# Attention in an eight-stage kernel: one output product for two heads, with row sums spread by TensorE

## The reference

```python
kv = _rmsnorm(k_pass_lat, kv_a_ln_w) @ kv_b_proj_w.T          # latent: 64 wide
scores = jnp.einsum('bhqd,bhkd->bhqk', q, k) * scaling
scores = jnp.where(causal[None, None], scores, NEG)
probs = jax.nn.softmax(scores.astype(jnp.float32), axis=-1).astype(q.dtype)
out = jnp.einsum('bhqk,bhkd->bhqd', probs, v)
out = out.transpose(0, 2, 1, 3).reshape(b, s, H * V_DIM)
return out @ o_proj_w.T
...
x = _layernorm(x + _L0_attn_ref(x, ...), axis=-1)
```

## Time and profile before

| | |
|---|---|
| Median of 3 runs | 815.58 us (813.26 to 816.98) |
| Span of the profiled execution, first to last instruction | 851.6 us |
| Mean granted TensorE clock | 0.982 |
| TensorE, VectorE, ScalarE, GpSimd busy | 92%, 65%, 46%, 32% |
| Attention loop in the profiled execution | about 72 to 413 us |

### The profile page before, as it was taken

The page is one execution under the profiler, slowest core; times in us unless marked ns, Lnnn a source line. Parts: engine busy times, 40 slices in busy tenths (PEclk is TensorE's granted clock), DMA queues, the critical chain, the costliest instruction groups (busy, mean ns, idle before and its releaser), DMA issues.

```text
span 851.6 us, 16159 instructions
## 1 busy us (share of the span) xinstructions
PE 786.6 (92%) x4635; PEld 660.7 (78%) x4635; DVE 556.9 (65%) x1423; ACT 394.8 (46%) x898; POOL 271.2 (32%) x357
## 2 busy tenths in 40 slices
PE   8998999999899999999879998899999799999957
PEld 7887877778787887777677877788897688888746
DVE  4324778877778787777345555468856387778536
ACT  1334656656565666655123343323333266666411
POOL 2004445534333232222345545524415100000241
PEclk9999999999999999999889999999999999999979
DMA  7449950000000000073176999687621335555321
GB/s 212 102 107 384 406 198 34 34 27 27 21 27 28 20 21 14 27 240 135 51 230 184 323 319 296 213 288 257 246 99 69 106 112 150 149 149 153 95 69 49
DMA packets 62881, 120.74 MB, mean 142 GB/s; under 512 B 18272, under 2 KB 32864, under 8 KB 62688
## 3 DMA queue, kind: packets, MB, share of 16 engines
q1 hardware_dynamic: 51824, 95.41, 35.2%
q0 software_dynamic: 7680, 21.51, 7.0%
q10 hardware_dynamic: 3312, 3.02, 1.0%
HBM read 76.13 MB, written 43.78 MB: 141 GB/s over the span
## 4 chain that ended last, share of the span: by engine, by line
PE 65%; DVE 11%; issue 11%; ACT 4%; POOL 3%; another core or an unknown queue 3%; DMA 2%; DVEq 0%; SPq 0%; ACTq 0%; POOLq 0%
PE scores L1627 9%; PE scores L1625 8%; PE scores L1626 8%; PE scores L1849 5%; PE acc_ps L2035 4%; PE misc_ps L1755 3%; PE probsT_ps L1762 3%; PE probsT_ps L1740 3%; PE misc_ps L1753 3%; DVE xT_lo L1096 3%; PE scores L1859 3%; PE acc_ps L1740 2%; PE probsT_ps L1979 2%; DVE neg_max L1090 2%
## 5 line engine op out<-in xcount | busy, mean ns | idle before, releaser
L826 ACT ACTIVATE area<-scores,neg_max 128x128 f32<-128x128 f32 (+7 forms) x128 | 94.9, 742 | 87.7 <-DVE neg_max L1090 85.5
L1090 DVE TENSOR_REDUCE neg_max<-scores 128x1 f32<-128x128 f32 (+7 forms) x128 | 95.8, 750 | 22.1 <-PE scores L1712 20.8
L708 POOL DMA_INDIRECT xe_d<-x_rows,send_i x64 | 64.1, 1001 | 55.5 <-ACT x_rows L850 38.5
L738 POOL DMA_INDIRECT ye_d<-area,home_i x64 | 61.4, 959 | 58.7 <-issue 28.6
L1849 PE MATMUL scores<-area 128*96 128x128 f32 x512 | 69.1, 279 | 2.1 <-issue 1.3
L1625 PE MATMUL scores<-kT_hi,weff_hi 128*128 128x512 f32 (+3 forms) x172 | 66.8, 388 | 0.9 <-ACT area L803 0.4
L1849 PEld LDWEIGHTS scores<-area 128*96 128x96 f32 x512 | 60.5, 166 | 5.2 <-issue 2.7
L1627 PE MATMUL scores<-kT_hi,weff_lo 128*128 128x512 f32 (+3 forms) x172 | 61.7, 359 | 0.0
L1626 PE MATMUL scores<-kT_lo,weff_hi 128*128 128x512 f32 (+3 forms) x172 | 61.5, 358 | 0.0
L696 POOL CAST weff_hi<-area 128x256 fp32r<-128x256 f32 x42 | 17.0, 406 | 136.5 <-PE scores L1712 88.8
L1755 PE MATMUL misc_ps<-xT_lo,xT_hi 128*128 128x512 f32 x144 | 58.4, 406 | 2.2 <-DVE xT_lo L1096 2.1
(11 more groups left out here) (290 smaller groups left out, 2081.4 us busy)
## 6 DMA issues: line engine op xcount, KB each, us to landing
area<-w SPq DMA_DIRECT2D x23, 512.0 KB, 4.0
area<-gate_up SPq DMA_DIRECT2D x24, 384.0 KB
xe_d<-area SPq DMA_DIRECT2D x8, 1088.0 KB, 11.3
ye_d<-area SPq DMA_DIRECT2D x8, 1024.0 KB, 16.7
area<-w SPq DMA_DIRECT2D x8, 1024.0 KB, 7.2
area<-ye_d SPq DMA_DIRECT2D x15, 512.0 KB, 5.2
area<-xe_d SPq DMA_DIRECT2D x28, 272.0 KB
area<-down SPq DMA_DIRECT2D x24, 192.0 KB
```

Source lines behind the costliest of these rows:

```text
L826: act.activation(row_of(n)[:, 0:L], score_bank(n)[:, 0:L], ACT.Exp, bias=neg_max[:, n % 4:n % 4 + 1], accum_out=rsum[:, s, k:k + 1]).then_ ...
L1090: dve.tensor_reduce(neg_max[:, n % 4:n % 4 + 1], score_bank(n)[:, 0:(n // HEADS + 1) * P], AX.X, ALU.max, negate=True).then_inc(max_ready, 1)
```

## The change

- `wvo` holds each head once: two neighbouring heads lie one above the other in its 128 rows (8 x 256 columns in place of 16 x 256).
- Once ScalarE has copied the context, VectorE adds the halves (`sum_context`): for heads 0 and 2 of a group into rows 0 to 63 of `ctxS`, for heads 1 and 3 into rows 64 to 127. Each of the two instructions has 64 partitions and 256 columns, one operand in PSUM and one in SBUF. This stands first in slot 0 two groups later.
- The division by the row sum moves ahead of the output product. `invert` writes each inverse in 64 copies (128 x 4 x 64), last in slot 3 of the group's own slots. TensorE transposes these copies (two transposes of 128x128, `spread_shares`, a new tenant of the PSUM seats) in slot 1 of the next group, ScalarE copies the result to SBUF (`copy_shares`, slot 2), and GpSimd multiplies `ctxS` by it (`share`, slot 1 of the group after).
- One output for a group: two products of 128 rows and 256 columns into one bank, in slot 2 two groups later. VectorE adds it to the residual with one plain addition in slot 3 (`add_out`).
- The copied context has one buffer in place of two; the context bank is free for the next group when the halves are added. Some semaphores are merged to make room for new ones.

The core of the diff:

```diff
-        wvo = cutA3(HEADS * HID)
+        wvo = cutA3(PAIRS * HID)
+        ctxS, shares = cutA3(3, HID), cutA3(3, HID)
+        rinv = cutA3(2, QUAD, RANK)
...
-                if spot % 2 and 0 <= G - 2:
-                    tenants.append(("out", QUAD * (G - 2) + spot // 2))
-        tenants += [("out", QUAD * (GROUPS - 1) + i) for i in range(QUAD)]
+                if spot == 3 and 0 <= G - 1 < GROUPS:
+                    tenants.append(("shares", G - 1))
+                if spot == 5:
+                    tenants += [("out", g) for g in outs_at(G)]
+        tenants += [("out", g) for g in outs_at(GROUPS + 1)]
...
+            def share(g):
+                pool.wait_ge(ctx_summed, 2 * g + 2)
+                pool.wait_ge(shares_done, g + 1)
+                pool.tensor_tensor(ctxS[:, g % 3, :], ctxS[:, g % 3, :], shares[:, g % 3, :], ALU.mult).then_inc(ctx_shared, 1)
...
             def copy_ctx(G):
                 act.wait_ge(ctx_step, blocks_to(G + 1))
-                if G >= 2:
-                    act.wait_ge(out_ready, QUAD * (G - 1))
-                act.copy(ctxT[:, G % 2, :], ctx_ps[:]).then_inc(ctx_copied, 1)
+                act.copy(ctxT, ctx_ps[:]).then_inc(ctx_copied, 1)
+
+            def copy_shares(g):
+                act.wait_ge(shares_ps, g + 1)
+                if g >= 3:
+                    act.wait_ge(ctx_shared, g - 2)
+                act.copy(shares[:, g % 3, :], seat_of("shares", g)[:, 0:HID]).then_inc(shares_done, 1)
...
-                dve.tensor_copy(wvo[:, bass.ds(2 * m * HID, 2 * HID)], misc[:]).then_inc(wvo_done, 1)
+                for b in range(2):
+                    ins = dve.tensor_copy(wvo[b * RANK:(b + 1) * RANK, bass.ds(m * HID, HID)],
+                                          misc[b * RANK:(b + 1) * RANK, b * HID:(b + 1) * HID])
+                ins.then_inc(wvo_done, 1)
...
-                dve.reciprocal(rinv[:, G % 3, :], rsum[:, G % 3, :]).then_inc(rinv_done, 1)
+                if G >= 2:
+                    dve.wait_ge(shares_ps, G - 1)
+                dve.reciprocal(rinv[:, G % 2], rsum[:, G % 3, :].unsqueeze(2).broadcast_to([P, QUAD, RANK])).then_inc(rinv_done, 1)
+
+            def sum_context(g):
+                dve.wait_ge(ctx_copied, g + 1)
+                if g >= 3:
+                    dve.wait_ge(out_ready, g - 2)
+                for b, other in ((0, 1), (1, 0)):
+                    mine_, its = (slice(k * RANK, (k + 1) * RANK) for k in (b, other))
+                    dve.tensor_tensor(ctxS[mine_, g % 3, :].rearrange("p (a n) -> p a n", a=2),
+                                      ctx_ps[mine_, :].rearrange("p (a b n) -> p a b n", a=2, b=2)[:, :, b, :],
+                                      ctxT[its, :].rearrange("p (a b n) -> p a b n", a=2, b=2)[:, :, b, :],
+                                      ALU.add).then_inc(ctx_summed, 1)
...
-                dve.scalar_tensor_tensor(x1[:, t, :], out_of(n), rinv[:, s, k:k + 1], x1[:, t, :] if h else x_in[:, t, :],
-                                         ALU.mult, ALU.add).then_inc(out_read, 1)
+                dve.tensor_tensor(x1[:, t, :], out_of(g), x_in[:, t, :] if first else x1[:, t, :],
+                                  ALU.add).then_inc(out_read, 1)
...
-                behind = n - 1 - 2 * QUAD
-                if 0 <= behind < TILES * HEADS:
-                    add_head(behind)
+                if i == 0 and 0 <= G - 2 < GROUPS:
+                    sum_context(G - 2)
+                if i == QUAD - 1:
+                    for g in outs_at(G):
+                        add_out(g)
...
-                if i == 1 and 0 <= G - 1 < GROUPS:
-                    invert(G - 1)
+                if i == QUAD - 1 and G < GROUPS:
+                    invert(G)
...
                     if G:
-                        pe.wait_ge(ctx_copied, G)
+                        pe.wait_ge(ctx_summed, 2 * G)
...
+            def spread_shares(g):
+                pe.wait_ge(rinv_done, g + 1)
+                take_seat("shares", g)
+                for a in range(2):
+                    last = pe.transpose(seat_of("shares", g)[:, a * P:(a + 1) * P],
+                                        rinv[:, g % 2, 2 * a:2 * a + 2].rearrange("p b r -> p (b r)"), ident[:])
+                last.then_inc(shares_ps, 1)
+
+            def output(g):
+                pe.wait_ge(ctx_shared, g + 1)
+                take_seat("out", g)
+                m = g % SETS * 2
+                for a in range(2):
+                    last = pe.matmul(out_of(g), ctxS[:, g % 3, a * P:(a + 1) * P], wvo[:, (m + a) * HID:(m + a + 1) * HID],
+                                     start=a == 0, stop=a == 1)
+                last.then_inc(out_ready, 1)
```

More of the change, by code:

```diff
@@ L109, in build @@
         rsum = sb("rsum", [P, 3, QUAD])
-        rinv = sb("rinv", [P, 3, QUAD])
         y = sb("y", [P, HID])
         sgd = sb("sgd", [P, 2, BANK])
-        ctxT = sgd
+        ctxT = sgd[:, 0, :]
         stats = sb("stats", [P, 6])
@@ L235, in build @@
         ld_head = [sem(f"ld_head{u}") for u in range(2)]
-        consts, made = sem("consts"), sem("made")
-        x_split, kv_ready, sq_done, keys_done, kT_ps, k_split, lat_split = (
-            sem(n) for n in ("x_split", "kv_ready", "sq_done", "keys_done", "kT_ps", "k_split", "lat_split"))
+        made = sem("made")
+        x_split, kv_ready, keys_done, kT_ps, k_split, ctx_summed, ctx_shared = (
+            sem(n) for n in ("x_split", "kv_ready", "keys_done", "kT_ps", "k_split", "ctx_summed", "ctx_shared"))
+        shares_ps, shares_done = sem("shares_ps"), sem("shares_done")
         weff_ps, weff_f32, weff_split, wvo_ps, wvo_done, qT_ps, qT_done = (
@@ L250, in build @@
         block = ctx.enter_context(nc.Block())
-        rows_zeroed, homes_made, home_step, home_done = (
-            sem(n) for n in ("rows_zeroed", "homes_made", "home_step", "home_done"))
+        rows_zeroed, home_step, home_done = (sem(n) for n in ("rows_zeroed", "home_step", "home_done"))
         zeroed, x1T_psd, x1T_done, logits_done, logits_read, chosen_done, place_done, place_read, send_done = (
@@ L401, in route_at, with out_slot, outs_at @@
             return route_places.get((G % SETS, place)) if SETS + 2 <= G < GROUPS else None
+        def out_slot(g):
+            return g + 2
+        def outs_at(G):
+            return [g for g in range(GROUPS) if out_slot(g) == G]
         tenants = []
@@ L418, in build @@
         LENT = pT + [acc, half[3]] + half[0:3]
-        long_rows = seat("out", TWO_OUTS)
+        long_rows = seat("block", blocks_to(SHORT // QUAD - 2))
         tail = seat("block", blocks_to(GROUPS - 1))
@@ L719, in pool_slot @@
                     split_q(n // 2 + 3)
+                if i == 1:
+                    for g in outs_at(G):
+                        share(g)
                 t, at = divmod(n - 2 * HEADS, HEADS)
                 if t == 0 and at == 0:
-                    pool.wait_ge(homes_made, 2)
+                    pool.wait_ge(consts1, 6)
                     pool.wait_ge(rows_zeroed, 16 * ROWS_ZEROED)
@@ L819, in exp_probs @@
                 if n == 4:
-                    act.wait_ge(lat_split, 2)
+                    act.wait_ge(keys_done, TILES + 3)
                 if row_before(n) >= 0:
@@ L855, in act_slot @@
             def act_slot(G, i, n):
+                if i == 2 and 0 <= G - 1 < GROUPS:
+                    copy_shares(G - 1)
                 for place in (2 * i, 2 * i + 1):
@@ L1027, in _ @@
             shared_act(1)
-            act.wait_ge(consts1, 6)
+            act.wait_ge(consts1, 8)
             for t in range(TILES // 2, TILES):
@@ L1100, in invert, with add_out @@
                 dve.wait_ge(probs_ready, QUAD * (G + 1))
-                dve.reciprocal(rinv[:, G % 3, :], rsum[:, G % 3, :]).then_inc(rinv_done, 1)
[L1103 to L1108, removed]
+                if G >= 2:
[11 more added lines that the diff above has]
+                                      ALU.add).then_inc(ctx_summed, 1)
+            def add_out(g):
+                t, first = g // SETS, g % SETS == 0
+                dve.wait_ge(out_ready, g + 1)
+                if first:
                     dve.wait_ge(ld_x, 32)
-                    dve.wait_ge(rinv_done, n // QUAD + 1)
                 else:
-                    dve.wait_ge(out_read, n)
-                dve.scalar_tensor_tensor(x1[:, t, :], out_of(n), rinv[:, s, k:k + 1], x1[:, t, :] if h else x_in[:, t, :],
-                                         ALU.mult, ALU.add).then_inc(out_read, 1)
+                    dve.wait_ge(out_read, g)
+                dve.tensor_tensor(x1[:, t, :], out_of(g), x_in[:, t, :] if first else x1[:, t, :],
+                                  ALU.add).then_inc(out_read, 1)
             def variance(k, src, eps, s=0):
@@ L1133, in attention_variance @@
             def attention_variance(t):
-                dve.wait_ge(out_read, (t + 1) * HEADS)
+                dve.wait_ge(out_read, (t + 1) * SETS)
```

(19 more changed lines are left out.)

18 lines of the change are left out of this document (8 added, 10 removed).

## The result

The changed kernel takes 868.69 us (median of 4 runs, 864.28 to 872.86), the kernel before 815.0 us (median of 4, 813.26 to 816.98). The ratio is 1.066, with a 95% interval of 1.0618 to 1.0702: slower by 54 us, where 48 were forecast.

What follows compares the result with a forecast made beforehand. The bound was taken as the chain between VectorE and ScalarE, TensorE close behind. 46.5 + 6.7 - 11.5 + 5.5 + 0.7 = +48 us on the 815.6 median gave 863 us, range 828 to 882, widened with rivals to 822 to 886.

Steps and rivals of the forecast that it cites:

- The place and the mechanism: At the turn of groups, reciprocal and sums on VectorE delay the lo copy and the chain behind it.
- W: VectorE's time at a turn, from the end of the last row maximum to the first lo copy; before, 1.6 us.
- The reciprocal: VectorE's inverse of 256 elements per partition, last in slot 3: 2.30 us, by a straight line from small sizes.
- The turn: Lo copy later at 30 turns, 46.5 us, plus normalisation statistics on top in 7 groups, 6.7 us.
- What comes back: Within a group VectorE is relieved of 1.15 us; a third counted, 11.5 us back, ends 0 and 34.5.
- ScalarE's copy: Copy of 128x256 from PSUM ahead of two hi copies in slot 2, 0.36 us; half counted, 5.5 us.
- TensorE's saving: Fewer output products save 0.64 us a group, 20.5 us in all; counted at nothing, as TensorE waits for the lump of VectorE work.
- GpSimd's: Product of 128x256 after the sums of slot 0, 0.73 us, done long before the output product; counted at nothing.
- The clock: Rival: pauses bring 1.2 GHz stretches in the first two tiles, 10 to 25 us more, say 885; chance 0.14.
- the path of the last group: At the loop's end, sums, GpSimd product, output product and addition, 2.9 us against 2.2: +0.7 us.
- Absorption into 82 us of idle time: Rival: VectorE's idle time in the loop takes up the 48 us of new work; 816 to 828, say 821; chance 0.10.
- A cheap reciprocal: Rival: at about 1 ns an element, 0.43 us, nothing at the turn is late; 805 us; chance 0.08.

Runs made afterwards that it cites:

- e7: The kernel before plus an unread wide reciprocal and unread sums of halves at the turn of groups, the context bank waiting for the sums: 874.99 us.
- e5: e2 with TensorE's spreading of the shares and ScalarE's copy of them each one slot later: 819.31 us.
- e2: The changed kernel with a 128x4 reciprocal on VectorE, its 64-fold copies made by GpSimd in slot 0 of the next group: 827.02 us.
- e8: e5 with the statistics of the normalisation one slot later, out of the turn of groups: 816.25 us.
- e4: The kernel before plus an unread 128x256 reciprocal at the end of slot 3 of every group: 835.9 us.
- e6: The kernel before plus two unread sums of halves at the start of slot 0, the context bank waiting for them: 827.64 us.
- e1: The changed kernel with a 128x4 reciprocal, then its 64-fold copy by VectorE, in the same place: 832.69 us.
- e3: The changed kernel with the wide reciprocal moved to the end of slot 1 of the next group, spreading and its copy one slot on: 871.38 us.

## Why the prediction was right

**The place and the mechanism** held. The time was 868.7 us, forecast 863; W grew by 41 us where the loop grew by 48, and e7 makes the loss with the block alone. That the number came so near is in part luck, as two terms of the sum were off by some 12 us each and cancelled.

**The reciprocal** was sized too long: 1.742 us, not 2.30, and outside the 2.2 to 2.4 us named as a sign of being right. From one element to 256 it is (1742 - 142)/255 = 6.3 ns an element, where the small sizes gave 8.3 to 8.7. The straight line through three points below 9 elements did not reach 256; that it is many times an addition's 1 ns did. By the Trainium skill, "VectorE: DVE Perf Modes", section "Walkthrough: the 8-slice pipeline in each mode", with eight passes, the estimate was 2.13 us for the stream alone; the measured 1.74 in all is less, and the measurement decides.

**The turn.** W before was taken as 1.6, it is 1.59. The forecast was 46.5 + 6.7 us for it (1.6 us a turn were worked out and 1.55 multiplied), measured 40.7: the shorter reciprocal takes off 0.56 x 30 = 17 us, and the other way the reading of the logits, which was not counted, stands in the way at 7 turns with some 0.4 us each.

**What comes back** is the term that failed: -11.5 us for the three additions saved within a group. In e5, which saves them too, W is 3.9 us above before and the time 4, and in after the groups at full clock grew by as much as W. Net of what the new chain may cost, nothing returned: it seems that the additions had stood in waits, all of them, not two thirds.

**ScalarE's copy** was put at 5.5 us, as a delay of the hi copies. e5 against e2 says 7.7, but mostly as time at 1.2 GHz; of the delay in every group little is seen. **TensorE's saving** was counted at nothing; e8 has it and runs as before. **GpSimd's** product, 728 ns, lies in 81 us of waiting for the sums.

So two errors of some 12 us, the long reciprocal and the relief, cancelled. **The clock** takes what the turns leave of the loop: its rival came true in part. The granted clock in the loop is 0.96 where it was 0.99 (27 us of the loop at 1.2 GHz, before 5), and one group of tile 3 has

```profile
192.34:207.09 14.75, 11.12 (x51) 8.82 (x50) 9.55 (x25) 5.46 (x12) 3.88 (x5) 0.77 0.05 19
```

at 0.77, 14.75 us where the same group took 9.55 at full clock before, against 2.5 and 1.9 us more in its two neighbours. In the group ahead of it, 12.25 us long, TensorE was busy 9.76 us, where before it was busy 9.51 of 9.80; just before the clock fell there it had paused for 1.3 and 1.1 us. By the Trainium skill, "TensorE: Matmul & The Clock Gate", "What's actually happening", the gate follows how busy the array was; the fall here came with idle time, as it says. No run isolated its price; an estimate is what the seven groups of after grew beyond their W, 18.2 - 10.5, some 8 us. The rival had put the clock in the first two tiles and as a case of its own, 873 us and more; in fact it came with the main one, and mostly in later tiles.

The turns and the clock together are 48 to 49 us. The loop shows 47.7, but the last group of before is 2 to 3 us longer in its profiled execution than in e4, e6 and e7, so the loop of before is shown a little too long. What is left of the 53.7 us lies behind the loop: after takes 413 us there (in a profiled execution 4 us above its median), e4, e6 and e7 take 406 to 407. Of that, 1.3 us is the path of the last group, from the last context copy to the last normalisation (6.4 us for 5.1), forecast at 0.7; the rest was not followed.

**The rivals.** Absorption into 82 us of idle time: that idle time is still there, 91 us of 389, and took up nothing beyond the first microsecond of each turn. A cheap reciprocal would not have made the kernel faster by 10 us as priced: e1 has 0.17 + 0.33 us in its place, about the rival's 0.43, and is at 833; e2 has 0.17 there and is at 827, and it takes two more moves to come level with before.

## What to carry to other kernels

Before adding work to an engine that is a quarter idle, look at what it is idle for: if it waits inside a chain that runs through it, only the length of that one wait is free (here about 1 us a turn), and the rest of a block is paid at full price, at every turn. Cut such a block, or move it to an engine off the chain, as GpSimd's 64-fold copies here; and where a small result is to be spread, invert first and copy after. Taking work away from an engine gains nothing while that work stands in its waits, and lumping together what was spread out can turn hidden work into a block, as the four products in one slot probably did. And look at a loop stretch by stretch, with its clock: e3 as a whole seemed to win nothing, and won 21 us in five tiles of eight.

## What was unexpected of the hardware

A reciprocal's time does not go on as its small sizes start: 142, 167 and 203 ns for 1, 4 and 8 elements per partition (8.3 to 8.7 ns for each one more), 1742 for 256 (6.3). A copy of 4 numbers in 64-fold into 256 takes VectorE 332 ns, a fifth of inverting the copies, and GpSimd 396 (e2):

```profile
L719 POOL COPY area<-few 128x256 f32<-128x256 f32 x32 | 12.7, 396 | 35.7 <-DVE few L1139 35.1
```

An addition on 64 partitions is no shorter than one on 128: 422 ns (L1138) and 418 (L1151) for 256 columns. And TensorE fell to 1.2 GHz in the middle of a busy loop, after pauses of 1.1 to 1.6 us (after, e2); pauses as long stand in before, at 106 and 328 us, without a fall.
